# A graph layer on one core: the first GIN product from one float32 product to three float32r products

## The reference

```
h  = relu(layernorm0(x))
xn = layernorm(h) * g1 + b1
aggr[dst] += relu(xn[src] + edge_attr)
g  = (1 + eps_gin) * xn + aggr
h2 = h + relu(g @ Wg1 + bg1) @ Wg2 + bg2
z  = layernorm(h2) * g2 + b2
out = x + h2 + gelu(z @ Wf1 + bf1) @ Wf2 + bf2      # Wf1: 128 x 512, Wf2: 512 x 128
```

## Time and profile before

| what | us |
|---|---|
| median of 3 runs | 1099.48 |
| lowest and highest run | 1099.12, 1101.86 |
| the profiled execution | 1099.35 |
| its span | 1097.5 |
| TensorE busy in the span (matmuls) | 1016.6 (93%) |
| ScalarE busy | 958.8 (87%) |
| VectorE busy | 939.4 (86%) |
| GpSimd busy | 909.4 (83%) |

### The profile page before, as it was taken

The page is one execution under the profiler, slowest core; times in us unless marked ns, Lnnn a source line. Parts: engine busy times, 40 slices in busy tenths (PEclk is TensorE's granted clock), DMA queues, the critical chain, the costliest instruction groups (busy, mean ns, idle before and its releaser), DMA issues. The chain is left out here.

```text
span 1097.5 us, 22877 instructions
## 1 busy us (share of the span) xinstructions
PE 1016.6 (93%) x6778; PEld 877.5 (80%) x6876; DVE 939.4 (86%) x3077; ACT 958.8 (87%) x2354; POOL 909.4 (83%) x649
## 2 busy tenths in 40 slices
PE   2247999999999999999999999999999999999998
PEld 1135888888888888888888888888888888878887
DVE  6568979999999989989989989989989989988642
ACT  1357989999999999999999999999999999989773
POOL 5679888899999899999899999989999999876720
PEclk9657999999999999999999999999999999999999
DMA  7777789655555555555554554554555554433211
GB/s 232 214 208 209 225 299 321 165 142 133 118 140 131 126 135 131 128 134 131 133 134 120 135 140 114 138 138 111 143 135 112 142 134 120 127 79 90 57 55 39
DMA packets 110163, 156.87 MB, mean 143 GB/s; under 512 B 24531, under 2 KB 50303, under 8 KB 110030
## 3 DMA queue, kind: packets, MB, share of 16 engines
q1 hardware_dynamic: 70054, 128.99, 37.9%
q0 software_dynamic: 37760, 25.66, 16.4%
q10 hardware_dynamic: 2216, 0.66, 0.3%
HBM read 90.61 MB, written 64.61 MB: 141 GB/s over the span
## 5 line engine op out<-in xcount | busy, mean ns | idle before, releaser
L433 POOL DMA_INDIRECT aggr_sums<-e_merged,e_index x196 | 331.3, 1690 | 68.2 <-issue 42.3
L934 PEld LDWEIGHTS p_out<-wf,n_act 128*128 128x128 f32 x3136 | 365.5, 192 | 3.6
L934 PE MATMUL p_out<-wf,n_act 128*128 128x128 f32 x3136 | 365.9, 275 | 0.1
L503 ACT ACTIVATE n_act<-p_f,bf1e_col 128x512 f32<-128x512 f32 x392 | 268.8, 686 | 47.7 <-PE p_f L890 47.5
L422 POOL DMA_INDIRECT e_x<-in_x,e_cols x196 | 231.3, 1180 | 50.1 <-issue 48.3
L890 PE MATMUL p_f<-n_z2T_high,wf_low 128*128 128x512 f32 x392 | 202.1, 515 | 7.8 <-ACT n_act L503 7.0
L494 ACT ACTIVATE n_z<-n_relu,n_shift,n_rstd 128x128 f32<-128x128 f32 x392 | 161.3, 485 | 26.9 <-DVE n_shift L682 26.9
L461 POOL TENSOR_TENSOR n_rstd<-n_var,minus_half 128x8 f32<-128x8 f32 x98 | 174.5, 1780 | 5.9 <-DVE n_var L703 3.6
L469 POOL TENSOR_TENSOR n_rstd<-n_var,minus_half 128x4 f32<-128x4 f32 x98 | 144.9, 1479 | 35.1 <-DVE n_var L835 35.0
L531 ACT ACTIVATE n_h<-n_relu,n_rstd 128x128 f32<-128x128 f32 x392 | 158.3, 406 | 0.0
L890 PE MATMUL p_f<-n_z2T_low,wf_high 128*128 128x512 f32 x392 | 155.2, 396 | 0.0
(11 more groups left out here) (95 smaller groups left out, 1742.5 us busy)
## 6 DMA issues: line engine op xcount, KB each, us to landing
n_x<-in_x SPq DMA_DIRECT2D x97, 256.0 KB, 2.7
n_aggr<-aggr_sums SPq DMA_DIRECT2D x97, 256.0 KB
out_dram<-n_out SPq DMA_DIRECT2D x97, 256.0 KB, 4.4
aggr_sums<-zeros SPq DMA_DIRECT2D x13, 1024.0 KB, 6.2
e_dst<-in_dst_rows SPq DMA_DIRECT2D x49, 256.0 KB, 4.2
e_attr<-in_attr SPq DMA_DIRECT2D x48, 256.0 KB, 3.2
aggr_sums<-zeros SPq DMA_DIRECT2D x6, 2048.0 KB, 9.0
e_x<-in_x,e_cols POOLq DMA_INDIRECT x196
```

What stands on the lines that cost most here:

```text
L433: nc.gpsimd.indirect_dma_start(out=aggr, out_offset=bass.IndirectOffsetOnAxis(ap=e_index[0:r, s, j:j + 1], axis=0), in_=e_merged[0:r, s, j ...
L503: nc.scalar.activation(n_act[:, k, :, 0:b.rows], p_f[k % 2][:, :, 0:b.rows], ACT.Gelu, bias=bf1e_col[:, k:k + 1]).then_inc(s_act, 1)
L934: last = nc.tensor.matmul(p_out[0:b.rows, j, :], n_act[:, k, j, 0:b.rows], wf2[:, k, :], start=False, stop=(k == KF - 1), skip_group_check ...
```

## The change

The transposed input of the first GIN product is kept as two float32r tiles: `n_inT_high`, which ScalarE rounds out of `p_in`, and `n_inT_low` = `p_in` - `n_inT_high`, which VectorE forms in the new `in_low`, right after `z2_low`, in every node step. `Wg1` is split into a high and a low part once, at the start. TensorE makes `p_g` of three float32r products (low weights by high input, high by low, high by high) that add up in PSUM, and waits for `s_inT_low` instead of `s_inT`. The transposes of the next block into `p_in` wait for the low part of this one, since VectorE now reads `p_in` too.

The place of `p_g` in the step is the same. The diff, without the lists of names:

```diff
@@ -204,7 +204,9 @@
         n_x, n_h, n_x2b = (sb(f"n_{n}", [P, 6, J, D]) for n in ("x", "h", "x2b"))
         n_aggr, n_relu, n_x2 = (sb(f"n_{n}", [P, 3, J, D]) for n in ("aggr", "relu", "x2"))
         n_z, n_zg, n_in, n_z2, n_out = (sb(f"n_{n}", [P, 2, J, D]) for n in ("z", "zg", "in", "z2", "out"))
-        n_inT, n_gT = (sb(f"n_{n}", [P, 2, J, P]) for n in ("inT", "gT"))
+        n_gT = sb("n_gT", [P, 2, J, P])
+        n_inT_high, n_inT_low = (sb(f"n_inT_{n}", [P, 2, J, P], F32R) for n in ("high", "low"))
+        wg1_high, wg1_low = (sb(f"wg1_{n}", [P, D], F32R) for n in ("high", "low"))
         n_z2T_high, n_z2T_low = (sb(f"n_z2T_{n}", [P, 2, J, P], F32R) for n in ("high", "low"))
         n_act = sb("n_act", [P, KF, J, P])
         n_stat = sb("n_stat", [P, 6, 2, J, 3])
@@ -549,7 +551,7 @@
                 if (b := node(2)) is not None:
                     act.wait_ge(s_tin, b.at + 1)
                     reached(act, s_g, b.at - 1)
-                    nc.scalar.activation(n_inT[:, b.slot(2), :, 0:b.rows], p_in[:, :, 0:b.rows],
+                    nc.scalar.activation(n_inT_high[:, b.slot(2), :, 0:b.rows], p_in[:, :, 0:b.rows],
                                          ACT.Identity).then_inc(s_inT, 1)
                 if 0 in halves and 1 in halves:
                     merged_rows(edge(3))
@@ -621,6 +623,7 @@
                 nc.vector.tensor_scalar(eps_col[:], eps_col[:], 1.0, None, ALU.add).then_inc(s_eps, 1)
                 dve.wait_ge(s_eps, 1)
                 nc.vector.tensor_scalar(b1e_col[:], b1_col[:], eps_col[:, 0:1], None, ALU.mult).then_inc(s_scaled_params, 1)
+                nc.vector.tensor_copy(wg1_high[:], wg1[:]).then_inc(s_wg1, 1)
                 nc.vector.tensor_scalar(wf1g[:], wf1[:], g2_col[:, 0:1], None, ALU.mult).then_inc(s_wf1, 1)
                 nc.vector.tensor_scalar(g1e_row[:], g1_row, eps_col[:, 0:1], float(D) ** 0.5, ALU.mult,
                                         ALU.mult).then_inc(s_scaled_params, 1)
@@ -650,6 +653,8 @@
                 dve.wait_ge(s_b1g, 1)
                 dve.wait_ge(s_wf1, 3)
                 nc.vector.tensor_tensor(wf1_low[:], wf1g[:], wf1_high[:], ALU.subtract).then_inc(s_wf1, 1)
+                dve.wait_ge(s_wg1, 1)
+                nc.vector.tensor_tensor(wg1_low[:], wg1[:], wg1_high[:], ALU.subtract).then_inc(s_wg1, 1)
                 dve.wait_ge(s_b2f, 1)
                 nc.vector.tensor_tensor(bf1e_col[:], p_f[0][:, :, 0], bf1_col[:], ALU.add).then_inc(s_bf1, 1)
                 nc.vector.tensor_tensor(bg1e_col[:], p_g[:, 0, 0:1], bg1_col[:], ALU.add).then_inc(s_bias, 1)
@@ -689,6 +694,14 @@
                     nc.vector.tensor_tensor(n_z2T_low[:, b.slot(2), :, 0:b.rows], p_z2[:, :, 0:b.rows],
                                             n_z2T_high[:, b.slot(2), :, 0:b.rows],
                                             ALU.subtract).then_inc(s_z2T_low, 1)
+
+            def in_low(node):
+                if (b := node(2)) is not None:
+                    dve.wait_ge(s_inT, b.at + 1)
+                    reached(dve, s_g, b.at - 1)
+                    nc.vector.tensor_tensor(n_inT_low[:, b.slot(2), :, 0:b.rows], p_in[:, :, 0:b.rows],
+                                            n_inT_high[:, b.slot(2), :, 0:b.rows],
+                                            ALU.subtract).then_inc(s_inT_low, 1)
 
             def relu_stats(node):
                 if (b := node(0)) is not None:
@@ -719,6 +732,7 @@
                                             ALU.mult, ALU.add).then_inc(s_evar0, 1)
                 shift(node)
                 z2_low(node)
+                in_low(node)
                 if c is not None:
 
 
@@ -874,6 +889,7 @@
             nc.tensor.matmul(p_f[1][:], mean_of[:], wf1g[:], start=True, stop=True).then_inc(s_wf1_mean, 1)
             pe.wait_ge(s_bias, 1)
             pe.wait_ge(s_wf1, 4)
+            pe.wait_ge(s_wg1, 2)
             pe.wait_ge(s_const, 8)
             pe.wait_ge(s_rows, 2)
 
@@ -897,10 +913,13 @@
                     pe.wait_ge(s_z2T_low, b.at + 1)
                     first_product(b, (0, 1))
                 if (b := fourth) is not None:
-                    pe.wait_ge(s_inT, b.at + 1)
+                    pe.wait_ge(s_inT_low, b.at + 1)
                     reached(pe, s_gT, b.at)
-                    nc.tensor.matmul(p_g[:, :, 0:b.rows], wg1[:], n_inT[:, b.slot(2), :, 0:b.rows],
-                                     start=True, stop=True).then_inc(s_g, 1)
+                    products = ((wg1_low, n_inT_high), (wg1_high, n_inT_low), (wg1_high, n_inT_high))
+                    for i, (weights, inT) in enumerate(products):
+                        last = nc.tensor.matmul(p_g[:, :, 0:b.rows], weights[:], inT[:, b.slot(2), :, 0:b.rows],
+                                                start=(i == 0), stop=(i == 2))
+                    last.then_inc(s_g, 1)
                 if (b := seventh) is not None:
                     first_product(b, (2, 3))
                 if (b := fourth) is not None:
@@ -920,7 +939,7 @@
                     last.then_inc(s_tz2, 1)
                 if (b := third) is not None:
                     pe.wait_ge(s_nin, b.at + 1)
-                    reached(pe, s_inT, b.at)
+                    reached(pe, s_inT_low, b.at)
                     for j in range(J):
                         last = nc.tensor.transpose(p_in[:, j, 0:b.rows], n_in[0:b.rows, b.slot(2), j, :],
                                                    ident[0:b.rows, 0:b.rows])
```

More of the change, by code:

```diff
@@ L219, in gnn_kernel @@
         p_f = [pb(f"p_f{i}") for i in range(2)]
-        (s_row_param, s_node_param, s_row_one, s_spread, s_rows_out, s_const, s_ones, s_eps, s_scaled_params, s_b1g, s_b2f, s_wf1, s_wf1_mean, s_bf1, s_bias, s_zeros, s_part, s_rows,
+        (s_row_param, s_node_param, s_row_one, s_spread, s_rows_out, s_const, s_ones, s_eps, s_scaled_params, s_b1g, s_b2f, s_wg1, s_wf1, s_wf1_mean, s_bf1, s_bias, s_zeros, s_part, s_rows,
          s_order_in, s_bounds, s_order, s_bad, s_flag) = (sem(f"s_{n}") for n in (
-             "row_param", "node_param", "row_one", "spread", "rows_out", "const", "ones", "eps", "scaled_params", "b1g", "b2f", "wf1", "wf1_mean", "bf1", "bias", "zeros", "part", "rows",
+             "row_param", "node_param", "row_one", "spread", "rows_out", "const", "ones", "eps", "scaled_params", "b1g", "b2f", "wg1", "wf1", "wf1_mean", "bf1", "bias", "zeros", "part", "rows",
              "order_in", "bounds", "order", "bad", "flag"))
@@ L237, in gnn_kernel @@
         (s_nstat, s_nrelu, s_nvar0, s_nstatu, s_nvar, s_nrstd, s_nshift, s_nz, s_nh,
-         s_nzg, s_nin, s_tin, s_inT, s_g, s_gT, s_gout, s_x2, s_stat2, s_var2, s_rstd2,
+         s_nzg, s_nin, s_tin, s_inT, s_inT_low, s_g, s_gT, s_gout, s_x2, s_stat2, s_var2, s_rstd2,
          s_x2b, s_z2, s_tz2, s_z2T, s_z2T_low, s_f, s_act, s_fout, s_nout) = (
@@ L241, in gnn_kernel @@
                 "stat", "relu", "var0", "statu", "var", "rstd", "shift", "z", "h",
-                "zg", "in", "tin", "inT", "g", "gT", "gout", "x2", "stat2", "var2", "rstd2",
+                "zg", "in", "tin", "inT", "inT_low", "g", "gT", "gout", "x2", "stat2", "var2", "rstd2",
                 "x2b", "z2", "tz2", "z2T", "z2T_low", "f", "act", "fout", "out"))
```

## The result

The changed kernel takes 1104.21 us, the median of 17 runs (1101.67 to 1106.56). The kernel before, run between them on the same chip, takes 1101.15 (1098.04 to 1105.76). The ratio is 1.0026, interval 1.0015 to 1.0038: **0.26% slower, where 0.28% faster was forecast**. The profiled execution of after took 1106.04 us.

The account below looks back on a forecast made before the run. TensorE was taken to set the pace, with ScalarE last to arrive in odd steps. 1099.4 - 2.5 (regular pairs) - 0.8 (tail) + 0.2 (start) = 1096.3 us; own range 1092 to 1100, whole range 1092 to 1112.

Parts of the forecast that it names:

- So 2 x 0.60 = 1.20 us a pair ... against 1.42 idle: it fits: VectorE: the added `n_inT_low` fits its idle time in each pair of steps, with 0.22 us to spare.
- rival A: GpSimd becomes the bound as VectorE's shifted work lengthens its gather issue and root: 0.25 us a pair, 1109 us, chance 0.30.
- TensorE's 0.16 us a block: TensorE: three float32r products take 0.70 us where the float32 `p_g` took 0.86, in each block.
- Odd step worth 0, gap 0.3: TensorE's odd step: k=3 still waits for ScalarE's gelu, gaining 0; the gap before it grows from 0.13 to about 0.3 us.
- rival B: Full gain: the gelu does not hold k=3 and each block gives 0.16 us; 1083.7 us, chance 0.04.
- Even step worth 0.065: TensorE's even step: the k=3 group starts at 618.875 instead of 618.94, 0.065 us a pair, 2.5 us over 38 pairs.
- The stated signs: In the profile after: ScalarE's `n_z2` waits for GpSimd's root in each pair; gather issue behind `n_in` takes 1.4 to 1.5 us.
- The new wait is never the first to bite: TensorE's `p_g` wait for `n_inT_low`: 3.5 us of cover or more; if lost, `n_z2T_low`, needed 1.5 us before, is late too.
- Clock, transposes into `p_in`, ScalarE's copy: TensorE's clock stays at 1.00, the transposes' wait for the low part is over by then, ScalarE's float32r copy costs 0.
- Tail: About 5 blocks without edge work at the end each gain 0.16 us, 0.8 us in all.
- Start: Two small VectorE operations on the 128x128 weights at the start cost 0.2 us, between 0 and 1.4.

Follow-up runs that it names:

- e3: The changed kernel with GpSimd's root for `n_z2` ahead of the scatters in the odd step; 1098.39 us against 1099.79 for before.
- e2: The kernel before with only VectorE's low-part subtraction added, its result unread and the float32 product kept; 1104.96 us against 1099.79 for before.
- e7: The kernel before with a VectorE memset of 760 columns where the low part would stand; 1106.74 us against 1100.25 for before.
- e12: The kernel before with GpSimd's root ahead of the scatters and ScalarE's `e_merged` copy behind gelu k=2; 1092.03 us against 1100.95 for before.
- e9: The changed kernel with GpSimd's root ahead of the scatters and ScalarE's odd-step `e_merged` copy behind gelu k=2; 1092.22 us against 1100.88 for before.
- e1: The changed kernel without the low part, its product reading the high part again; 1097.84 us against 1099.79 for before.
- e5: The changed kernel with the low parts of blocks 0 to 2 formed ahead of VectorE's wait for gathered rows; 1104.8 us against 1100.25 for before.
- e8: The kernel before with a GpSimd memset of 256 columns ahead of the scatters in each odd step; 1103.11 us against 1100.25 for before.
- e4: The kernel before with GpSimd's root ahead of the scatters in the odd step; 1099.08 us against 1099.79 for before.
- e10: The kernel before with ScalarE's odd-step `e_merged` copy behind gelu k=2, GpSimd's order unchanged; 1133.6 us against 1100.88 for before.

## Why the prediction was wrong

The forecast was 1096.3 us and faster; measured is 1104.2 and slower, outside the forecast's own 1092 to 1100 and inside the whole range. **The step that failed is the one on VectorE: "So 2 x 0.60 = 1.20 us a pair ... against 1.42 idle: it fits".** As room on VectorE that is true: `e_sum` still waits 7.9 us over the 29 pairs, 0.27 us a pair where 0.22 was to be left, and at 591 us busy in e3 the pair is the short one. But the sum took "it fits" for "it costs nothing": it has no term for what the shift does on GpSimd, though rival A, some lines below, had worked out that the shift alone brings `n_in` over the gather issue and the root into the `e_sum` pair. That was given 0.30 against 0.53 because the time could come back elsewhere. Some does (the gather that took 1.51 us in the earlier trace rows takes 1.12 at 620.44), but 0.39 back is less than the 0.53 at the other gather and the 0.53 at the root. What the runs showed in place of that nothing: the shift alone makes the pair 20.50 us (e2) and 20.51 (e7) where before has 20.36, and the root, which ended 0.69 us ahead of `n_z2` before, ends 0.04 us ahead of it in after, with `n_z2` itself 0.2 us late. e2 and e7 show the shift as the cause, e3 the root as its place.

Point by point:

- **TensorE's 0.16 us a block:** right; 0.69 us for the three products, e12 against e9 gives 0.16 for the odd step, and the steps without edge work at the end give it in full (see the tail below).
- **Odd step worth 0, gap 0.3:** right; 9.58 us before and after, gap 0.31. e9 closes this gap by moving ScalarE's copy alone, so ScalarE was what held k=3. That rules out rival B.
- **Even step worth 0.065:** right where nothing else interferes, 10.78 to 10.72 in e1, e3 and the 6 undisturbed pairs of after. It is also the whole gain to be had there.
- **Rival A:** the meetings, their places and the need at `n_z2` were right; the price of 0.25 us a pair was too high. The root ends 0.2 us past the need, which is as far as `e_sum` can push it, and a disturbed even step is 0.19 us longer than an undisturbed one. Set against before, 27 of 33 pairs lose 0.14 and 6 gain 0.06: 0.10 us a pair on average, 38 x 0.10 = 3.8 us where 38 x 0.25 = 9.5 was said. Of its two terms only the root counted: the longer gather issue (1.59 us) is there in e3 too, without a loss. The stated signs were half right: `n_z2` is late by 0.2 us in each such pair, but as the root's end and `n_z2`'s start lie 0.04 apart, the table of waits from 300 to 900 us has no row for it. The chain has: GpSimd 56%.
- **"The new wait is never the first to bite":** wrong, 12.0 us over three waits in the first blocks. Without cost, by e5.
- **Clock, transposes into `p_in`, ScalarE's copy:** as forecast; 1.00 in the regular part, no wait on either.
- **Tail:** half seen. The steps without edge work are 9.44, 9.44 and 9.29 us long before and 9.28, 9.28 and 9.13 after: 0.16 each, TensorE's whole gain. The two steps behind them give only 0.11 and 0.01, so 0.6 us in all instead of 5 x 0.16 = 0.8. In after these are, from one first `p_f` product to the next:

```profile
1043.56 0.48 PE L906 MATMUL p_f<-n_z2T_high,wf_low 128*128 128x512 f32 x1
...
1052.84 0.48 PE L906 MATMUL p_f<-n_z2T_high,wf_low 128*128 128x512 f32 x1
```

and before:

```profile
1036.14 0.48 PE L890 MATMUL p_f<-n_z2T_high,wf_low 128*128 128x512 f32 x1
...
1045.58 0.48 PE L890 MATMUL p_f<-n_z2T_high,wf_low 128*128 128x512 f32 x1
```

- **Start:** unsettled. At the relu `n_gT` of the block with number 16 after is 2.1 us behind before (245.09 against 242.99), but e7 and e8, which have no weights to split, are 1.7 and 1.6 behind as well, and e4 is 4.0. There is one profiled execution of each, so the 0.2 us was not measured.

The Trainium skill (GPSIMD Engine Reference, Specifications) names the contention on the shared interfaces with two-input instructions of VectorE. The traces agree on where it falls: `n_inT_low`, with one input in SBUF, begins 0.18 us behind the root at 638.25 and the root keeps its 1.60 us, while the `e_sum` instructions, which lengthen it, have two. The 2.13 for 1.60 us is the traces' own. In e7 the memset itself reads nothing, and the long root ends 1.57 us after `e_sum` begins, as in the others.

## What to carry to other kernels

Idle time of an engine says whether new work fits, not what its shift does: look up which instructions behind it will now start beside another engine's, and whether one of those ends within some tenths of a microsecond of its reader. If such a near miss exists, first move that instruction away (here the root ahead of the scatters), and only then spend the slack. And before the engine that is the bound is made faster, check that nobody else closes the loop: here ScalarE's unbroken 11.30 us took nearly all of TensorE's 0.32 us a pair back.

## What the runs showed of the hardware

GpSimd's root of 128x4, standing behind a scatter, reacts to VectorE's first `e_sum` instruction (a multiplication of 128x512 with both inputs in SBUF) only if that begins soon enough after it. Begun 0.17 to 0.58 us behind the root's start, it made the root 1.74 to 2.15 us long; begun 0.59 us behind or later, up to 1.08, it left the root at 1.59 to 1.61. The long root has no fixed length: it ended 1.57 us after `e_sum` began, so it is longest just before the border and then falls back to 1.60. Two pairs of e2, one on each side; GpSimd and VectorE:

```profile
844.03 2.15 POOL L470 TENSOR_TENSOR n_rstd<-n_var,minus_half 128x4 f32<-128x4 f32 x1
...
926.07 1.60 POOL L470 TENSOR_TENSOR n_rstd<-n_var,minus_half 128x4 f32<-128x4 f32 x1
```

```profile
844.61 0.69 DVE L799 TENSOR_TENSOR e_sum<-e_z,rows 128x512 f32<-128x512 f32 x1 [0.37 <-ACT e_z L495]
...
926.66 0.72 DVE L799 TENSOR_TENSOR e_sum<-e_z,rows 128x512 f32<-128x512 f32 x1 [0.38 <-ACT e_z L495]
```

So 0.01 us decides over 0.55 us of GpSimd's time, and on the far side it is `e_sum` that takes 0.03 longer. If the root begins later still, it meets the second `e_sum` instruction: in e10 that starts 0.73 us behind the first, and the root, begun 0.49 behind the first, ended 2.30 behind it, which is 1.57 behind the second. What the root does in the 0.58 us in which a meeting counts isn't shown; the scatter ahead of it lasts until 0.53 us after its start (617.07 + 1.58 = 618.65 in after).
